# The opening of a fused cross-attention and mixture-of-experts kernel: order of its loads, squares and first projections, and constant products

## The reference

```python
xl = layernorm(x)                        # per row of 512
q = Wq @ xl + bq;  k = Wk @ ctx + bk;  v = Wv @ ctx + bv      # per batch, 256 x 512
dot = einsum('bhdt,bhds->bhts', q, k) / sqrt(16)
dot = mask * dot - (1 - mask) * 1e6
out = softmax(dot) * mask @ v
x = x + out
flat = layernorm(x)                      # 2048 tokens of 512 in the second part
g, u = flat @ shared_gate.T, flat @ shared_up.T
shared = sigmoid(g) * u @ shared_down.T
logits = flat @ router_w.T               # top 2 of 8 experts, softmax weights
routed = sum over the token's 2 experts of weight * (sigmoid(xb @ wg.T) * (xb @ wu.T)) @ wd.T   # bf16
x = x + shared + routed
```

## Time and profile before

| | us |
|---|---|
| median of 3 runs | 650.21 (649.96 to 651.75) |
| the profiled execution | 651.81 |
| its span, first to last instruction | 649.7 |

### The profile page before, as it was taken

The page is one execution under the profiler, slowest core; times in us unless marked ns, Lnnn a source line. Parts: engine busy times, 40 slices in busy tenths (PEclk is TensorE's granted clock), DMA queues, the critical chain, the costliest instruction groups (busy, mean ns, idle before and its releaser), DMA issues.

```text
span 649.7 us, 12595 instructions
## 1 busy us (share of the span) xinstructions
PE 608.8 (94%) x4110; PEld 260.9 (40%) x4110; DVE 511.6 (79%) x983; ACT 469.2 (72%) x657; POOL 359.9 (55%) x494
## 2 busy tenths in 40 slices
PE   4799999999999999999999999889999999999987
PEld 3554332332332332332332332224554466666533
DVE  2478999999999999999999999995528745454477
ACT  3653899899899899899899788885442276667511
POOL 5458464575575575575575453423653577777410
PEclk9989999999999999999999999999999999999999
DMA  8641534634544534634533533115698533333178
GB/s 286 189 145 46 145 97 120 180 109 137 156 127 141 166 118 142 182 108 137 149 107 89 150 110 82 67 41 131 160 219 198 105 102 107 105 101 106 58 230 312
DMA packets 64990, 88.66 MB, mean 136 GB/s; under 512 B 12624, under 2 KB 45264, under 8 KB 63904
## 3 DMA queue, kind: packets, MB, share of 16 engines
q1 hardware_dynamic: 60032, 68.72, 34.4%
q0 software_dynamic: 4896, 19.14, 12.1%
HBM read 63.75 MB, written 32.74 MB: 149 GB/s over the span
## 4 chain that ended last, share of the span: by engine, by line
PE 75%; DVE 11%; issue 6%; ACT 4%; DMA 2%; POOL 1%; SPq 1%; ACTq 0%; POOLq 0%; DVEq 0%
PE PS L1100 17%; PE PS L1000 11%; PE PS L1376 9%; PE PS L1070 8%; DVE MX L1010 7%; PE PS L1836 7%; PE PS L859 5%; PE PS L1899 4%; PE PS L1650 3%; ACT E L1084 2%; PE PS L854 2%; PE PS L1005 1%; PE PS L947 1%; PE PS L1797 1%; PE PS L943 1%
## 5 line engine op out<-in xcount | busy, mean ns | idle before, releaser
L1010 DVE TENSOR_REDUCE MX<-PS 128x1 f32<-128x512 f32 x512 | 323.1, 683 | 17.3 <-PE PS L1000 15.5
L1084 ACT ACTIVATE E<-PS 128x1024 f32<-128x1024 f32 x256 | 253.7, 1019 | 32.2 <-PE PS L1070 28.1
L1000 PE MATMUL PS<-BIG 53*128 53x512 f16 x512 | 129.0, 384 | 12.3 <-DVE MX L1010 10.7
L1100 PE MATMUL PS<-E,BIG 128*32 128x512 f32 x1024 | 136.4, 605 | 1.0 <-ACT E L1084 0.9
L1070 PE MATMUL PS<-BIG 55*128 55x512 f16 x512 | 101.7, 382 | 5.4 <-ACT E L1084 0.6
L893 POOL TENSOR_TENSOR ML<-BIG,ML 128x512 f32<-128x512 f32 x30 | 38.3, 1276 | 102.8 <-ACT BIG L869 102.6
L1000 PEld LDWEIGHTS PS<-BIG 53*128 53x128 f16 x512 | 34.4, 93 | 134.5 <-DVE MX L1010 120.6
L1858 DVE SCALAR_TENSOR_TENSOR E<-WP,PS 128x352 bf16<-128x352 f32 x39 | 20.3, 521 | 45.5 <-ACT WP L1848 45.5
L869 ACT ACTIVATE BIG<-PS,BIG 128x256 f32<-128x256 f32 x64 | 35.7, 560 | 27.8 <-PE PS L854 16.4
L1836 PE MATMUL PS<-BIG,CT 128*128 x312 | 52.9, 313 | 1.0 <-DVE WP L1411 1.0
L1918 POOL DMA_INDIRECT scr_ys<-SW,bvB x39 | 38.2, 981 | 19.3 <-DVE SW L1911 10.1
(11 more groups left out here) (272 smaller groups left out, 908.9 us busy)
## 6 DMA issues: line engine op xcount, KB each, us to landing
scr_parts<-WP SPq DMA_DIRECT2D x96, 128.0 KB
BIG<-scr_parts SPq DMA_DIRECT2D x64, 192.0 KB
BIG<-in_we POOLq DMA_DIRECT2D x8, 1088.0 KB, 14.1
scr_u<-ML SPq DMA_DIRECT2D x32, 256.0 KB, 2.7
X<-in_x SPq DMA_DIRECT2D x8, 512.0 KB, 6.2
CT<-in_ctx SPq DMA_DIRECT2D x8, 512.0 KB, 3.8
ML<-scr_u SPq DMA_DIRECT2D x16, 256.0 KB
ML<-scr_recs SPq DMA_DIRECT2D x16, 256.0 KB
```

Source lines behind the costliest of these rows:

```text
L1000: e.matmul(PS[:, yi[name] % 3, :], QK[rows, qb(u), 0, j0 + jj, 128 * tt:128 * tt + 128], QK[rows, qb(u), 1, j0 + jj, :], start=True, stop= ...
L1010: e.tensor_reduce(MX[:, g % 2, c:c + 1], PS[:, yi[name] % 3, :], AX.X, ALU.max)\
L1084: e.activation(E[:, st, 2 * jj:2 * jj + 2, :], PS[:, slot(name):slot(name) + 2, :], ACT.Exp, scale=1 / 1024).then_inc(s["rc"], 1)
L1100: ins = e.matmul(PS[32 * hh:32 * hh + 32, avb, :], VT[:, b % 2, st, 4 * (g % 4) + hh, :], E[:, st, hh, :], start=(st == 0), stop=(st == 3))
```

## The change

- The k weights are issued before the source of batch 0.
- `load_one` (x, source, mask of batch 1) is issued from ScalarE's queue, after the first normalise, instead of from SyncE's after the shared weights.
- The filling of two constant rows for the mask goes from `dve_aux` to the very start of VectorE's queue.
- The two halves of unit 0's k go to banks 4 and 6 and don't wait for the copies of q out of 3 and 5.
- The squares of the shared weights go behind those of batch 1 and the second half of unit 1's q on ScalarE; their sum "z" goes behind unit 1's k and v on TensorE; their factor goes ahead of batch 1's ratio on GpSimd, and their split behind more of GpSimd's work.
- Batch 1's reciprocal (`invert`) goes behind the first six maxima on VectorE, its `columns` behind the second k split on GpSimd.
- `load_x(2)` goes behind the loads of unit 0's parts.
- Constant products of 256 columns: 20 at the start of TensorE's queue, 14 before batch 1's sum, 32 between "z" and the first score.

```diff
-        mring.append((-1.26, ("z",)))
+        mring.append((-1.0, ("z",)))
         def slot(name):
-            return 3 + 2 * (zi[name] % 2)
+            return 3 + 2 * (zi[name] % 2) + (name[:2] == ("k", 0))
             e.dma_start(bqkc[:, :], bqk).then_inc(s["w"], 16)
+            e.dma_start(WQ[:, 1, :, :], wqkv[:, 1]).then_inc(s["w1"], 16)
             load_source(e, 0)
-            e.dma_start(WQ[:, 1, :, :], wqkv[:, 1]).then_inc(s["w1"], 16)
-            sp.at(2 * b - 6 + .02, load_x(b))
+            sp.at(-1.5 if b == 2 else 2 * b - 6 + .02, load_x(b))
-        sp.at(-18, load_one)
+        act.at(-10.5, load_one)
         def dve_aux(e):
-            e.memset(ef[0:8, 0:512].bitcast(HF), 32000.0)
-            e.memset(ef[0:8, 512:1024].bitcast(HF), 32768.0)
+        def dve_rows(e):
+            e.memset(ef[0:8, 0:512].bitcast(HF), 32000.0)
+            e.memset(ef[0:8, 512:1024].bitcast(HF), 32768.0)
+        dve.at(-20, dve_rows)
+        def keep_clock(n):
+            def mm(e):
+                e.wait_ge(s["id"], 6)
+                for _ in range(n):
+                    e.matmul(PS[:, AVB, 0:256], identb[:, :], ident[:, :].bitcast(BF), start=True, stop=True)
+            return mm
+        pe.at(-20, keep_clock(20))
+        pe.at(-1.2755, keep_clock(14))
+        pe.at(-.995, keep_clock(32))
         # balance: invert and columns
-            dve.at(when_at[name] + .6 * IT, invert)
+            dve.at(-.9 if b == 1 else when_at[name] + .6 * IT, invert)
-            pool.at(when_at[name] + .32 * IT, columns)
+            pool.at(-.89 if b == 1 else when_at[name] + .32 * IT, columns)
         # split_shared: squares, factor, lower
-            act.at(-1.9, squares)
+            act.at(-1.4, squares)
-            pool.at(when_at[name] + .4 * IT, factor)
+            pool.at(-1.3, factor)
-                pool.at(-.9, f)
+                pool.at(-.8, f)
         # project_qk: mm
-                    take_slot(e, name)
+                    if w or i == 0:
+                        take_slot(e, name)
```

## The result

| | before | after |
|---|---|---|
| median | 650.09 us (649.25 to 652.94, 8 runs) | 647.19 us (645.64 to 657.84, 8 runs) |
| the profiled execution | 651.81 | 645.64 |
| its span | 649.7 | 643.5 |

The change makes the kernel faster: the ratio to the kernel before, run beside it, is 0.994 (95% interval 0.9922 to 0.9957), that is 3.9 us. One of the eight executions after, 657.84 us at a mean clock of 0.979, is left out of that ratio. A second set of runs of the same code gave 0.9925 (0.9891 to 0.996), that is 4.9 us.

What follows compares the result with a forecast made beforehand. The start of the first score matmul at 37.00 us was taken as the bound; two paths, TensorE's stream and k's store, meet at 31.9, gaining 5.1: 650.2 - 5.1 = 645.1 us, range 643.0 to 648.8.

Steps and rivals of the forecast that it cites:

- k weights: Opening loads: k weights issued one place earlier, at about 2.27, land at 6.5 us, so norms may start at 7.2.
- The norms' length: TensorE's norm matmuls, 3.57 us before; norms and small product kept at 4.28, putting the first q projection at 11.65.
- The first rival: Opening: the 20 products lift the clock through the norms, T 15.5 to 16.5, first score 30, time 643.2; chance 0.12.
- T: End of the first k projection on TensorE, 22.54 us before; forecast 18.1, with bounds 17 to 19.2.
- k in its own banks: First k projection on TensorE no longer waits for q's copy; the 1.35 us gap before 18.76 goes.
- The shared squares: ScalarE ends them at T + 9.55, TensorE's groups end by T + 9.8; first score T + 13.7, before T + 14.45.
- The store of k: SyncE's store and load back of split k: last issue 28.2, first score not before 31.4 to 32.7 us.
- The second batch's source: Load issued from ScalarE behind the first normalise, at 11.4; lands at 21 us or sooner, needed at 21.5.
- The rival in which it lands late: Second batch's source, issued from 12.3, lands at 24.7, 3.2 us late; first score 35.1, time 648.3; chance 0.12.
- The gain given back: Behind the first score, waits on work that moves less lose 3 to 5 us; time 649.5; chance 0.09.
- A difference carries over: Last step of the sum: the 5.1 us gained at the first score comes off the median too, 650.2 to 645.1.
- The slower rival: Second batch's sum to first score at 1.2 GHz: 7.2 us more, first score 39.1, time 652.3; chance 0.04.

Runs made afterwards that it cites:

- the second profile: Profile of the changed kernel itself, run again without any edit on the chip of three other kernels: 646.84 us, ratio 0.9925 to the kernel before.

## Why the prediction was right, and where its sizes were off

The time forecast, 645.1, is 2.1 below the median measured, and the first score, forecast at 31.9, came at 30.57 and 30.88. The order of the links held, and the two paths to the first score did meet. That the time came out so close is in part luck: the first score moved by 1.0 to 1.3 us more than forecast, and 1.2 to 3.5 us less of it than forecast arrived in the medians and ratios. And one part of the mechanism, what a low clock costs, was wrong; it is taken up last.

- **k weights.** Landing forecast at 6.5; issued at 2.26, they landed 4.5 us later, at 6.8. The source landed at 8.1 instead of 8.65. Norms at 7.51 for 7.35. Right, and putting the weights back cost 1.7 to 2.0 us of first score.
- **The norms' length.** Taken at 3.57; they took 1.95. The term of the sum was mis-sized because the record before had them at the slow clock, and the 20 products had lifted it. The first rival named that. But it only half came true in the first profile: the clock held through the norms, fell within the stretch from 9 to 12 us (0.61) and was 0.50 from 12 to 15. So q's input, ready at 10.9, bound its start, and the forecast of 11.65 was 0.7 late. q's copy followed at 14.66, 1.4 earlier than forecast. In the second profile T was 15.94, outside the forecast's 17 to 19.3 and inside the rival's 15.5 to 16.5. The rival's step from there, a k that lands quickly and a first score at 30, failed: the first score came at 30.88, and with T at 14.2 at 30.99.
- **k in its own banks.** In the first profile T was 17.36 against 18.1. The step that gave the banks their 1.35 us was too simple. With the old banks the gap was only 0.55 us in this order, and 1.3 us of slow clock on k and v stood beside it. That the clock rises earlier without the gap is likely and not shown, since it rose at different times in two executions of one code too.
- **The shared squares.** They ended at 26.63 (26.44 + 0.19), where T + 9.55 is 26.9 with the measured T; the four groups ended at 26.25, where T + 9.8 is 27.2, and no idle stretch over 0.52 us lies between T and the first score (0.71, and 1.40 ahead of the first score, in the second profile). The prediction priced a constant product at 0.108 us and the 32 at 3.45, where its two rows give 0.105 ((0.75 - 0.54) / 2); from the first of them to the first score it was 3.59. The kernel with the squares back shows that the whole move is worth some 4 to 5 us. In it lies more than the 3.30 us of idle time: the slow clock on the groups behind it.
- **The store of k.** VectorE ended the splits at 20.14 for 21.4, SyncE the mask stores at 18.26 for 19.1, and the last load was issued at 26.41 for 28.2. k landed by 30.57, in the second profile at 30.88, that is 3.6 us after its last issue (27.29). Forecast was 31.4 to 32.7. The bound of 4.5 from issue to landing held in the second profile; over all kernels whose first score waits for k the time was 2.8 to 4.7 us, the most in the one with two products beside each score (31.69 - 27.00).
- **The second batch's source.** Issued at 9.55, landed 10.8 us later, at 20.35, when it was needed at 20.46. The row of after:

```profile
X<-in_sd SPq DMA_DIRECT2D x1, 768.0 KB, 12.2
...
CT<-in_ctx ACTq DMA_DIRECT2D x1, 512.0 KB, 10.8
```

The rival in which it lands late, with 12.4 us from 12.3, is false; it failed at the issue time, 9.55 instead of 12.3, since ScalarE issues while an activation runs. It was a near thing all the same: with T at 14.2 this landing is what TensorE waits for. Before, the source took 12.4 us. In the Trainium skill, "DMA: Bandwidth & Descriptors", section "Queues, rings and completion order", engines take turns between queue rows; the 1.6 us that the source gained while the shared expert's last load took 12.2 us (11.7 before) agree with it, but the source also was asked for later and behind fewer bytes, so these rows don't prove it. The section "Issuing engines are not separate DMA queues" says that another issuing engine saves only the time of the issue. The kernel with the loads on SyncE shows that saving, 2.2 us at the start of the mask stores, and that here it lies on the path.

- **The gain given back.** Not in the profiles: from the first score to the last scatter it took 582.0 us before and 582.1 and 581.9 after, and the second k split moved by 6.1, forecast 4.4.
- **A difference carries over.** This step of the sum was off by more than the others. The first score moved by 6.4, more than the 5.1 forecast, the medians of the two kernels only by 2.9 and the ratio by 3.9 us (4.9 in the second set). The execution of before that was profiled lay 1.7 us above its median, that of after 1.5 below. And the two profiles of the same code differ by 1.5 us, nearly all of it behind the last scatter. Single executions carry a spread of that size which belongs to no edit. Whether it accounts for the whole gap between 6.1 to 6.4 us of first score and 2.9 to 4.9 us of time stays open, since the kernel before was profiled only once.
- **The slower rival.** Here the working was wrong although the outcome was right. It let the low clock cost the stretch between the second batch's sum and the first score, 7.2 us at most, and it took the 32 products for a price of 3.45 us. The runs show another picture. In this order the products are nearly free, because k lands about as late as they end, and what they stand against is larger than anything in that sum: 9.3 us without the 32 and 17.8 without all, paid behind the first score, in scores that start at the slow clock and stay there for 22 and 48 us. The clock's fall in a short idle stretch was there to be read the earlier trace rows, and the forecast itself left a wait of up to 4 us between the shared sum and k's landing. By this sum a kernel without the products would have been forecast near 645, where 665 was measured. A wait of TensorE had to be priced by what the clock does behind it, not by its own length.

"TensorE: Matmul & The Clock Gate" of the Trainium skill, section "What's actually happening", puts the cost of the ramp to full clock below 1% of a typical kernel's span. The measured loss of the order without products is 1.6% against before, and 2.4% against the changed kernel (1.0163 / 0.9925), so for this kernel the measurement says otherwise. What it cost here is no single ramp but a low level that lasted for 22 and 48 us.

What stays open: why the four groups before had come back to full clock by the first score (0.99 from 36 to 52 us) and the scores of the two kernels above did not. In both cases TensorE was busy all the time up to the rise; the instructions differ, single-precision projections of 256 columns in the one, half-precision scores of 512 columns and products in the other. Nor was it tried how few of the 32 products would do. Nor does the length of an idle stretch alone say whether the clock falls: behind the 14 products it fell after 1.41 us in the kernel with the products alone (0.50 from 28 to 30 us), and it held over 1.83 us in the kernel with ten more (1.00 from 18 to 23).

## What to carry to other kernels

Before taking work or a wait out of an opening, look where TensorE will idle next, and at which clock the long loop behind it starts: here a start at the low clock cost two to six times the idle stretch of 4.7 and 3.1 us ahead of it. Products of constants placed in a wait that must be served anyway cost next to nothing here, and they pay when they reach to the end of the wait; take them out once to see whether the matmul behind them would start earlier. When a part is taken back to measure it, take back with it the moves that were made for it, and price a difference from medians of runs made side by side, since single executions of one code differed by 1.5 us.

## What the runs showed of the hardware

- The low clock can keep itself: busy in all of 16 us, TensorE stayed at 0.50 from 36 to 52 us in two kernels, and in one of them until about 79 us, in a stream in which a score takes 0.60 and three products 0.82.
- Sixteen matmuls of one column took 1.95 us at the high clock (with ten more products, granted 1.00) and 3.57 to 3.58 in stretches where the projections behind them ran at the low rate, so this group scales with the clock.
- ScalarE issued three DMAs in 0.43, 0.69 and 0.60 us while its activations ran on; on SyncE the same three took 1.32, 0.84 and 0.54, and delayed what stood behind them.
- On another chip every kernel took some 37 us more, the kernel before too, without any change of the program. In the experts' part the granted clock was 0.85 where it had been 1.00 (500 to 590 us), and TensorE was also idle for 20 of the 90 us where it had been for 1.
